# Turning softmax probabilities by halves of 49 rows, in two goes of six blocks

## The chip, the cores and the metric

The kernel runs on one core of one Trainium2 chip. Its time is the device time of one execution in microseconds (us); lower is better. The core has TensorE (PE: matrix products out of SBUF into the eight PSUM banks; PEld is its loading of weights), VectorE (DVE), ScalarE (ACT), GpSimd (POOL, which does not read PSUM) and the DMA queues. Each engine works through its own instructions in order and meets the others at semaphores.

## What is computed

Four layers one after the other on x of 32 images, 56 x 56 pixels, 96 channels, float32. The first and third are of no matter here (a depthwise convolution along the pixels with two products; a 7 x 7 depthwise convolution that is part of the third layer). The second and the fourth are the same transformer block on windows of 7 x 7 pixels with six heads of 16 channels:

```python
h = _ln(x, g1, b1)
h = jnp.roll(h, shift=(-SHIFT, -SHIFT), axis=(1, 2))
h = h.reshape(B, nHw, WS, nWw, WS, C).transpose(0, 1, 3, 2, 4, 5).reshape(B * nHw * nWw, WS * WS, C)
q, k, v = jnp.moveaxis((h @ w_qkv + b_qkv).reshape(-1, N, 3, nh, hd), 2, 0)
attn = jax.nn.softmax(jnp.einsum('wqhd,wkhd->whqk', q, k) * scale, axis=-1)
out = jnp.einsum('whqk,wkhd->wqhd', attn, v).reshape(-1, N, C) @ w_proj + b_proj
...
x = shortcut + out
h2 = _ln(x, g2, b2)
return x + jax.nn.gelu(h2 @ w_fc1 + b_fc1, approximate=False) @ w_fc2 + b_fc2
```

The third layer has the attention too, with a bias and a mask, and no second half.

## The kernel before

The program is a row of passes: `scan_pass` (first layer), `window_pass` for "L1" (second layer, here called the second pass), `conv_pass`, `window_pass` for "L2" (third layer) and `window_pass` for "L3" (fourth layer, here called the fourth pass). In `window_pass` the flag `mlp` is true for L1 and L3; the change touches only what stands under it.

A chunk is one row of eight windows of one image, 8 x 49 = 392 pixels; there are 32 x 8 = 256 chunks in a pass. All four engines go over the chunks in step (`over_chunks`, with 24 steps to a turn of the hardware loop), each with a step function written out by hand: `mlp_step` for L1 and L3. A step is software-pipelined: in step t, TensorE makes keys, queries, values and scores of chunk t (`st.f`), turns the probabilities, takes heads and the projection of chunk t-1 (`st.k`), the hidden products of chunk t-2 (`st.m`) and the output products of chunk t-3 (`st.n`). `st.wait(name, lag)` waits until a semaphore has counted the chunk `lag` back. `hold` puts such a wait on an instruction of its own.

The windows are worked in pairs, the even window on partitions 0 to 48 and the odd one on 64 to 112, so that a tile spans `SPAN` = 113 rows. The probabilities stand in PR as 113 query rows by 24 head slots of 64 columns: window pair by window pair (four), six heads each. The product of probabilities and values (`heads`, L1069) needs them with the keys on the partitions, so TensorE turns them against the identity (`turn`, L1006): a block is two heads of a window pair, 113 rows by 113 columns, loaded as weights, while 113 columns of the identity stream through. Twelve blocks make a chunk (`PAIRS` x `G`, 4 x 3). They are turned in three lots of four, a lot to one PSUM bank: lot 0 to bank 4, lot 1 to bank 5, lot 2 to bank 4 again, which waits for `pt0`, the copy of lot 0 to the tile PT. VectorE makes that copy (L1388), ScalarE those of lots 1 and 2 (L1235). `probs0` and `probs1` are the two halves of the exponential (L1251), twelve head slots each.

TensorE's step around it is: keys and queries (L1013), output products 0 and 1 (`output`, L1105; each waits for the low parts that GpSimd makes, L1501), turn of lot 0, the sums of squares (`variances`, L990), output product 2, turns of lots 1 and 2, the spreading of 1/std to the channels (`spread`, L1000; it waits for ScalarE's logarithm L1226 and exponential L1230 of the variances), values (L1028), in L3 the turn to pixels (L1097), heads (L1069), two hidden products (L1013), scores (L1052), the turn of the heads (L1076), the third hidden product and the projection (L1087). Bank 5 is also that of the heads and of the projection, bank 4 that of the turned heads.

## Time and profile before

| what | us |
|---|---|
| runs | 11234.27, 11250.2, 11244.17 |
| median | 11244.17 |
| profiled execution, its own time | 11245.42 |
| its span in the trace | 11243.6 |
| TensorE busy in the span | 10697.9 (95%) |
| ScalarE, VectorE, GpSimd busy | 7724.4 (69%), 7313.1 (65%), 5856.8 (52%) |

The mean granted clock of TensorE is 0.978. In the views, a row of a timeline gives the start and the length of a group in us from the span's start; the length of a group of TensorE instructions overlaps with the next group, since products are pipelined, so starts are the better measure. A product in float32 that is no turn appears as two rows (x48 for 24 instructions), a turn as one. "113*96" before a shape is the rows and columns of the array that are used.

### The profile page before, as it was taken

Reading aid. Unit: us, or ns where it says so; the run is one execution under the profiler, and the core shown is the slowest. Engines: PE = TensorE matmul, PEld = TensorE weight load, DVE = VectorE, ACT = ScalarE, POOL = GpSimd, SP = SyncE. Lnnn points to the kernel's source line nnn. Section 1 sums busy time; section 2 is a strip of 40 time slices with the busy share of each in tenths; the row PEclk is TensorE's granted clock in tenths of the full one; section 3 lists DMA queues with packets and bytes.
Section 4 is the critical chain, followed back from the end, with each engine's and each line's share of the span. In section 5 each row is a group of like instructions: output and inputs, shape, how many; then the busy total and the mean of one; then the engine's idle time right before and its main releaser. Section 6 shows DMA issues by size and latency. Waiting matters only on the chain. (4 is left out here: it accounts for less than half of the span.)

```text
span 11243.6 us, 395055 instructions
## 1 busy us (share of the span) xinstructions
PE 10697.9 (95%) x160084; PEld 8550.1 (76%) x160084; DVE 7313.1 (65%) x12431; ACT 7724.4 (69%) x13429; POOL 5856.8 (52%) x7492
## 2 busy tenths in 40 slices
PE   6999998999999999998989999998999999999999
PEld 4666666777777777777767777776888888888888
DVE  4555555777777777773467676766666666666666
ACT  4555554777777777774357676765777777777777
POOL 2333334777777777771034444443555555555555
PEclk9999998999999999999989999998999999999999
DMA  2111111222222222225633333332111111111110
GB/s 60 51 46 51 46 42 36 52 52 52 52 52 52 52 52 52 52 52 173 215 80 79 76 80 76 80 77 51 26 26 26 25 25 26 26 26 26 25 25 23
DMA packets 1105555, 617.35 MB, mean 55 GB/s; under 512 B 864635, under 2 KB 1076550, under 8 KB 1099688
## 3 DMA queue, kind: packets, MB, share of 16 engines
q1 hardware_dynamic: 1091368, 552.46, 20.4%
q10 hardware_dynamic: 12288, 38.54, 1.0%
q8 instruction: 1317, 21.58, 0.8%
q14 instruction: 582, 4.77, 0.1%
HBM read 307.18 MB, written 282.75 MB: 52 GB/s over the span
## 5 line engine op out<-in xcount | busy, mean ns | idle before, releaser
L1501 POOL TENSOR_TENSOR L_HdL<-L_Hd,L_HdH 128x392 fp32r<-128x392 f32 x1536 | 1576.8, 1027 | 280.9 <-POOL L_HdH L1499 279.3
L1006 PE MATMUL banks<-L_ident,L_PR 113*113 113x113 f32 x9216 | 1201.7, 267 | 1.2 <-DVE L_X L1407 0.7
L1006 PEld LDWEIGHTS banks<-L_ident,L_PR 113*113 113x113 f32 x9216 | 1143.6, 180 | 67.2 <-DVE L_X L1407 9.8
L1235 ACT COPY L_PT<-banks 113x452 f32<-113x452 f32 x1792 | 886.1, 538 | 397.7 <-PE banks L1006 394.3
L1251 ACT ACTIVATE L_PR<-L_SX 113x588 f32<-113x588 f32 x1536 | 1088.5, 709 | 86.5 <-DVE L_SX L1379 10.2
L1069 PE MATMUL banks<-L_VB,L_PT 113*49 113x34 f32 x36864 | 1064.8, 213 | 2.0 <-ACT L_PT L1235 1.0
L1373 DVE TENSOR_REDUCE L_MX<-banks 113x12 f32<-113x588 f32 x1024 | 783.6, 765 | 433.5 <-PE banks L1052 433.5
L1069 PEld LDWEIGHTS banks<-L_VB,L_PT 113*49 113x49 f32 x36864 | 1016.7, 126 | 25.5 <-issue 1.8
L1490 POOL CAST L_XNH<-L_XN 97x392 fp32r<-97x392 f32 x512 | 448.6, 876 | 1105.4 <-DVE L_XN L1420 1105.4
L1499 POOL CAST L_HdH<-L_Hd 128x392 fp32r<-128x392 f32 x1536 | 784.6, 511 | 459.9 <-issue 425.6
L1052 PEld LDWEIGHTS banks<-L_KX,L_QT 32*49 32x49 f32 x36864 | 565.1, 119 | 333.9 <-issue 331.8
L1549 POOL COPY L_XN<-L_XR 96x392 f32<-96x392 f32 x256 | 149.6, 584 | 1278.3 <-DMA L_XR<-L_norm 1193.8
L1379 DVE TENSOR_TENSOR L_SX<-banks,L_MX 113x588 f32<-113x588 f32 x1024 | 788.8, 770 | 35.3
L1052 PE MATMUL banks<-L_KX,L_QT 32*49 32x98 f32 x36864 | 726.1, 249 | 50.1 <-issue 49.1
L1028 PE MATMUL banks<-L_Wv,L_XN 97*49 97x48 f32 x24576 | 730.2, 213 | 0.0
L1105 PE MATMUL banks<-L_HdH,L_W2H 128*97 128x392 f32 x1536 | 593.6, 386 | 121.2 <-POOL L_HdL L1501 121.1
L1087 PE MATMUL banks<-L_OT,L_Wp 97*97 97x392 f32 x1536 | 691.8, 532 | 14.5 <-ACT L_OT L1282 1.1
L1028 PEld LDWEIGHTS banks<-L_Wv,L_XN 97*49 97x49 f32 x24576 | 634.5, 127 | 78.2 <-issue 3.0
L1286 ACT ACT_TABLE_LOAD x512 | 656.9, 1283 | 9.4
L1274 ACT ACT_TABLE_LOAD x512 | 656.9, 1283 | 9.2
L1388 DVE COPY L_PT<-banks 113x452 f32<-113x452 f32 x512 | 321.9, 629 | 515.1 <-PE banks L1006 515.1
L1439 DVE SCALAR_TENSOR_TENSOR L_X<-banks,L_fc2b,L_X 97x392 f32<-97x392 f32 x512 | 320.3, 626 | 515.1 <-PE banks L1105 515.1
(249 smaller groups left out, 28455.0 us busy)
## 6 DMA issues: line engine op xcount, KB each, us to landing
L_X<-after_L SPq DMA_DIRECT2D x768, 147.0 KB
after_L<-L_X SPq DMA_DIRECT2D x512, 147.0 KB
conv_T<-L_norm_by_phase SPq DMA_DIRECT2D x96, 512.0 KB, 3.3
L_norm_by_phase<-L_XP SPq DMA_DIRECT2D x512, 84.0 KB, 2.1
scan_XT<-in_x SPq DMA_DIRECT2D x32, 1176.0 KB, 6.9
L_norm<-L_XA SPq DMA_DIRECT2D x256, 147.0 KB, 1.9
L_conv<-conv_D ACTq DMA_DIRECT2D x96, 392.0 KB, 3.0
L_XR<-L_norm SPq DMA_DIRECT2D x256, 147.0 KB, 2.4
```

The source lines that it names most:

```text
L1006: mm = pe.transpose(bank(TURN[a])[0:SPAN, (k % 4) * SPAN:(k % 4 + 1) * SPAN], PR[:, st.v if lag else st.u, 2 * k:2 * k + 2, :].rearrange(" ...
L1028: mm = pe.matmul(bank(VALUES_BANK)[HALF * e:HALF * e + TOK, q * G * HD:(q + 1) * G * HD], XN[:, st.u, q * TOK:(q + 1) * TOK], Wv[0:C + 1, ...
L1052: mm = pe.matmul(bank(g)[p0:p0 + TOK, q // 2 * 2 * TOK:(q // 2 + 1) * 2 * TOK].rearrange("c (e k) -> c e k", e=2), QT[rows, st.u, q * TOK: ...
L1069: mm = pe.matmul(bank(HEADS_BANK)[p0:p0 + TOK, col:col + VW], PT[:, st.v, q // 2 * G + g, p0:p0 + TOK], VB[:, st.v, q, g, :], start=True, ...
L1087: pe.matmul(bank(PROJ_BANK)[0:C + 1, 0:CH], Wp[0:C + 1, :], OT[:, st.v], start=mlp, stop=True).then_inc(s["proj"], 1)
L1235: act.copy(PT[:, st.v if lag else st.u, 4 * a:4 * a + 4, :].rearrange("c k q -> c (k q)"), bank(TURN[a])[0:SPAN, 0:4 * SPAN]).then_inc(s[f ...
L1251: act.activation(PR[:, u, a, 0:TOK], SX[:, u, a], ACT.Exp).then_inc(s[f"probs{half}"], 1)
L1274: act.preload_act_table_set(GELU)
L1373: dve.tensor_reduce(mx, src, AX.X, ALU.max).then_inc(s[f"rowmax{half}"], 1)
L1379: dve.tensor_tensor(dst, src, spread, ALU.subtract).then_inc(s[f"centred{half}"], 1)
L1499: pool.tensor_copy(HdH[:, u, j].bitcast(F32R), Hd[:, u, j]).then_inc(s[f"hd_high_{j}"], 1)
L1501: pool.tensor_tensor(HdL[:, u, j].bitcast(F32R), Hd[:, u, j], HdH[:, u, j], ALU.subtract).then_inc(s[f"hd_parts_{j}"], 1)
```

## The change

In L1 and L3 `turn` gives way to `turn_halves`. Each block of 113 x 113 is turned as two: the 49 rows of the even window, from partitions 0 to 48, into bank 4, and the 49 rows of the odd window, from partitions 64 to 112, into bank 5. Each has 49 rows and 113 columns of PR as weights and 49 columns of the identity as stream, and writes 49 columns. There are two goes of six blocks, twelve turns each, the first behind `probs0`, the second behind `probs1` and `pt0`, in place of lots of four, four and four. Both goes use both banks. Each go has one copy, 588 elements on each of 113 partitions in place of 452: VectorE's for the first, ScalarE's for the second, written around the unused columns of PT (`by_window`). The wait for `x1` moves ahead of the first go, since it writes bank 5 now. The waits for `probs0` and `pt0` become held waits. L2 keeps `turn` with three lots.

```diff
+        names += [f"{n}{a}" for n in ("turned", "pt") for a in range(2 if mlp else 3)] + ["heads", "rsum", "normed", "heads_t", "ot", "proj", "x1"]
+        HALVES = slice(4, 6)
+        HP = PAIRS * G // 2
+        def turned_halves():
+            return PS[0:SPAN, HALVES, 0:HP * TOK].rearrange("c e (k q) -> c e k q", q=TOK)
+        def by_window(t):
+            return bass.AP(t.tensor, t.offset, [t.ap[0], [HALF, 2], [SPAN, HP], [1, TOK]])
...
+                def turn_halves(st, a):
+                    for k in range(HP * a, HP * a + HP):
+                        for e in range(2):
+                            rows = slice(HALF * e, HALF * e + TOK)
+                            mm = pe.transpose(PS[0:SPAN, HALVES.start + e, (k % HP) * TOK:(k % HP + 1) * TOK],
+                                              PR[rows, st.v, 2 * k:2 * k + 2, :].rearrange("c h k -> c (h k)")[:, 0:SPAN], ident[rows, rows])
+                    mm.then_inc(s[f"turned{a}"], 1)
...
                     if st.k:
-                        st.wait("probs0", 1)
-                        turn(st, 0)
+                        st.wait("x1", 2)
+                        hold(pe, s["probs0"], st.value(1), passed)
+                        turn_halves(st, 0)
                     if normed:
                         variances(st)
                     if st.n:
                         output(st, 2).then_inc(s["fc2"], 1)
                     if st.k:
-
-                        st.wait("x1", 2)
                         st.wait("probs1", 1)
-                        turn(st, 1)
-                        st.wait("pt0", 1)
-                        turn(st, 2)
+                        hold(pe, s["pt0"], st.value(1), passed)
+                        turn_halves(st, 1)
...
+                def pt_halves(st, a):
+                    st.wait(f"turned{a}", 1)
+                    act.copy(by_window(PT[:, st.v, HP * a:HP * a + HP, :]), turned_halves()).then_inc(s[f"pt{a}"], 1)
...
-                        pt_copy(st, 1)
-                        pt_copy(st, 2)
+                        pt_halves(st, 1)
```

VectorE's copy is changed in the same way (`pt_copy(st, 0)` to `pt_halves(st, 0)`). Lines move by some twenty: `turn_halves` is L1025 in the changed kernel, the output products L1124, the variances L1000, the spreading L1010.

TensorE in a step of L3, from the last row of output product 1 to the spreading, as it stands before (HdH and W2L are high and low parts of the hidden layer and its weights, SQ the squares, J the averaging matrix, RS the 1/std, PICK the spreading matrix):

```order
L1105 MATMUL banks<-L_HdH,L_W2L 97x392
L1006 MATMUL banks<-L_ident,L_PR 113x113 x4
L687 REGISTER_ALU
L990 MATMUL banks<-L_SQ,L_J 32x98 x8
L1105 MATMUL banks<-L_HdH,L_W2H 97x392
L1105 MATMUL banks<-L_HdL,L_W2H 97x392
L1105 MATMUL banks<-L_HdH,L_W2L 97x392
L1006 MATMUL banks<-L_ident,L_PR 113x113 x8
L1000 MATMUL banks<-L_RS,L_PICK 96x98 x8
```

The same place on TensorE in the changed kernel:

```order
L1124 MATMUL banks<-L_HdH,L_W2L 97x392
L1025 MATMUL banks<-L_ident,L_PR 113x49 x12
L687 REGISTER_ALU
L1000 MATMUL banks<-L_SQ,L_J 32x98 x8
L1124 MATMUL banks<-L_HdH,L_W2H 97x392
L1124 MATMUL banks<-L_HdL,L_W2H 97x392
L1124 MATMUL banks<-L_HdH,L_W2L 97x392
L1025 MATMUL banks<-L_ident,L_PR 113x49 x12
L1010 MATMUL banks<-L_RS,L_PICK 96x98 x8
```

Four turns ahead of the variances and eight behind the last output product have become twelve of half the height and 49 columns out at each place; nothing else has moved.

ScalarE in the same step, from the logarithm to the rounding of XN2, before:

```order
L1226 ACTIVATE L_LV<-banks,L_eps 64x392
L1230 ACTIVATE L_RS<-L_LV 64x392
L1235 COPY L_PT<-banks 113x452 x2
L1264 CAST L_XN2H<-L_XN 97x392
L1244 COPY L_VB<-banks 49x24x16
```

and in the changed kernel:

```order
L1243 ACTIVATE L_LV<-banks,L_eps 64x392
L1247 ACTIVATE L_RS<-L_LV 64x392
L1272 COPY L_PT<-banks 113x2x6x49
L1284 CAST L_XN2H<-L_XN 97x392
L1261 COPY L_VB<-banks 49x24x16
```

Two copies have become one with more elements, at the same place.

## Rows read from the trace of the kernel before

**Rows 1.** The page, busy time, share of the span and instructions of each engine:

```profile
PE 10697.9 (95%) x160084; PEld 8550.1 (76%) x160084; DVE 7313.1 (65%) x12431; ACT 7724.4 (69%) x13429; POOL 5856.8 (52%) x7492
```

**Rows 2.** Windows: us, busy of PE, PEld, DVE, ACT, POOL, clock, DMA, GB/s:

```profile
2800.00:5100.00 2300.00, 2183.75 (x38968) 1796.08 (x38955) 1660.14 (x2864) 1728.89 (x2876) 1664.57 (x2330) 0.99 0.24 52
...
8000.00:11243.00 3243.00, 3195.18 (x52345) 2740.07 (x52343) 2147.03 (x3634) 2515.51 (x4376) 1759.08 (x2185) 0.99 0.10 25
```

**Rows 3.** Waits, 8100 to 11100 (L3): total us, times, longest:

```profile
ACT L_XN2H L1264 <- DVE L_XN L1417: 198.9, 226, 0.9
...
PEld banks L1013 <- issue: 116.3, 226, 4.0
...
PEld banks L1087 <- ACT L_OT L1282: 78.7, 226, 0.4
```

**Rows 4.** Waits, 2200 to 5000 (L1):

```profile
PEld banks L1105 <- POOL L_HdL L1501: 174.2, 210, 1.2
```

**Rows 5.** Timeline of one chunk in L3: start, length, engine, line, operation, count:

```profile
9004.04 0.34 PE L1105 MATMUL banks<-L_HdH,L_W2L 128*97 128x392 f32 x1
...
9004.22 0.56 PE L1006 MATMUL banks<-L_ident,L_PR 113*113 113x113 f32 x4
...
9004.70 0.87 PE L990 MATMUL banks<-L_SQ,L_J 96*32 96x98 f32 x16
...
9005.62 0.58 ACT L1226 ACTIVATE L_LV<-banks,L_eps 64x392 f32<-64x392 f32 x1 [0.18 <-PE banks L990]
...
9005.95 0.34 PE L1105 MATMUL banks<-L_HdH,L_W2L 128*97 128x392 f32 x1
...
9006.13 0.95 PE L1006 MATMUL banks<-L_ident,L_PR 113*113 113x113 f32 x8
9006.24 0.53 ACT L1230 ACTIVATE L_RS<-L_LV 64x392 f32<-64x392 f32 x1
...
9007.02 0.92 PE L1000 MATMUL banks<-L_RS,L_PICK 32*96 32x98 f32 x16
...
9007.87 0.94 PE L1028 MATMUL banks<-L_Wv,L_XN 97*49 97x48 f32 x32
...
9009.80 1.37 PE L1069 MATMUL banks<-L_VB,L_PT 113*49 113x34 f32 x48
```

**Rows 6.** Timeline of one chunk in L1:

```profile
4006.77 1.03 POOL L1501 TENSOR_TENSOR L_HdL<-L_Hd,L_HdH 128x392 fp32r<-128x392 f32 x1 [0.18 <-POOL L_HdH L1499]
...
4007.85 0.42 PE L1105 MATMUL banks<-L_HdH,L_W2H 128*97 128x392 f32 x1 [0.45 <-POOL L_HdL L1501]
...
4010.20 0.34 PE L1105 MATMUL banks<-L_HdH,L_W2L 128*97 128x392 f32 x1
...
4010.50 0.53 ACT L1230 ACTIVATE L_RS<-L_LV 96x392 f32<-96x392 f32 x1
...
4011.26 0.93 PE L1000 MATMUL banks<-L_RS,L_PICK 32*96 32x98 f32 x24
```

**Rows 7.** Timeline of PE in L3, windows that end at 9007.10 and at 9007.20:

```profile
9006.83 0.26 PE L1006 MATMUL banks<-L_ident,L_PR 113*113 113x113 f32 x1
9007.02 0.33 PE L1000 MATMUL banks<-L_RS,L_PICK 32*96 32x98 f32 x2
...
9007.02 0.41 PE L1000 MATMUL banks<-L_RS,L_PICK 32*96 32x98 f32 x4
```

**Rows 8.** Weight loads by line, 8100 to 11100: ns min/median/max, array rows*columns:

```profile
L1006 PEld LDWEIGHTS banks<-L_ident,L_PR x2708: 174/179/313, 8101.2 to 11091.3; 113*113 113x113 f32 x194
...
L1069 PEld LDWEIGHTS banks<-L_VB,L_PT x10848: 121/126/126, 8105.0 to 11095.5; 113*49 113x49 f32 x198
...
L1076 PEld LDWEIGHTS banks<-L_ident,L_O x904: 123/126/128, 8108.5 to 11098.1; 113*96 113x96 f32 x181
...
L1000 PEld LDWEIGHTS banks<-L_RS,L_PICK x3616: 154/159/161, 8102.3 to 11092.2; 32*96 32x96 f32 x191
```

**Rows 9.** The page, costliest groups: busy us, mean ns, idle before:

```profile
L1379 DVE TENSOR_TENSOR L_SX<-banks,L_MX 113x588 f32<-113x588 f32 x1024 | 788.8, 770 | 35.3
```

More of the change, by code:

```diff
@@ L839, in window_pass @@
                  "centred0", "centred1", "probs0", "probs1"]
-        names += ["turned0", "turned1", "turned2", "pt0", "pt1", "pt2", "heads", "rsum", "normed", "heads_t", "ot", "proj", "x1"]
+        names += [f"{n}{a}" for n in ("turned", "pt") for a in range(2 if mlp else 3)] + ["heads", "rsum", "normed", "heads_t", "ot", "proj", "x1"]
         if mlp:
@@ L1060, in heads @@
                     st.wait("pt1", 1)
-                    st.wait("pt2", 1)
                     if not mlp:
+                        st.wait("pt2", 1)
                         st.wait("ot", 2)
@@ L1384, in centre, with pt_halves @@
                     subtract(st, half)
-                def pt_copy(st, a):
+                def pt_halves(st, a):
                     st.wait(f"turned{a}", 1)
-                    dve.tensor_copy(PT[:, st.v, 4 * a:4 * a + 4, :].rearrange("c k q -> c (k q)"), bank(TURN[a])[0:SPAN, 0:4 * SPAN]).then_inc(s[f"pt{a}"], 1)
+                    dve.tensor_copy(by_window(PT[:, st.v, HP * a:HP * a + HP, :]), turned_halves()).then_inc(s[f"pt{a}"], 1)
                 def over_sums(st):
@@ L1432, in mlp_step @@
                     if st.k:
-                        pt_copy(st, 0)
+                        pt_halves(st, 0)
                     if st.n:
```

## The prediction

> **What bounds the kernel now.** I read the page's busy shares first: TensorE is busy 95% of the span, the next engine 69% [rows 1]. By stage, the two passes that the change touches hold it at 0.95 and 0.99 of the time, at a granted clock of 0.99, which is the 2.4 GHz level [rows 2]. Whatever TensorE takes longer or shorter on these passes therefore counts, unless a wait takes the difference. So I read the waits next. In the fourth pass every wait of TensorE is a short one behind its own work: for the turned heads (78.7 us over 226 chunks) and before the keys (116.3 us) [rows 3]; the view has no wait of it around the turning of the probabilities. In the second pass there is one more: the output product waits for GpSimd's low parts, 174.2 us in 210 waits [rows 4]. The timeline shows that this is a ring: GpSimd ends the second low part at 4007.80 (6.77 + 1.03), TensorE starts the output product at 4007.85, goes through the first turn, the variances, the output's last third, the second turn and the spreading (start 4011.26), VectorE makes XN from the spread factors, and GpSimd's splitting starts again from XN [rows 6]. Both turns lie inside that ring, so in the second pass, too, their time is the chunk's time.
>
> How much room is behind the turns? In the fourth pass (rows 5) the variances start at 9004.70, the logarithm at 9005.62, the exponential ends at 9006.77, and the spreading, which waits for it, starts at 9007.02. A semaphore takes about 0.06 us here (4007.80 to 4007.85 in rows 6), so the spreading has 0.19 us of room. In the second pass the exponential ends at 4011.03 against 4011.26, the same. **The second turn can be shortened by 0.2 us at most before the chain of logarithm and exponential ends last**; the first turn stands ahead of the variances, so it moves that chain with it at full price.
>
> **What the turns cost now.** From the start of the last output product to the start of what follows: first turn 9004.04 to 9004.70, 0.66 us; second turn 9005.95 to 9007.02, 1.07 us [rows 5]; in the second pass the second turn takes 1.06 (4010.20 to 4011.26) [rows 6]. Together 1.73 us for each chunk. Eight turns take 0.95 us as one group with the last one lasting 0.26, so they start (0.95 - 0.26) / 7 = 0.099 us apart [rows 5, 8].
>
> What sets these 0.099 us? Two things could: the 113 columns that stream, or the 113 columns of probabilities that are loaded as weights. The change cuts the stream to 49 columns and leaves the load at 113. So this is the question on which all hangs. Load times grow with the number of columns: 49 columns 126 ns, 96 columns 159, 113 columns 179 [rows 8], which is (179 - 126) / 64 = 0.83 ns for a column, about 0.094 us for 113. The group that turns values by heads separates load from stream: L1069 loads 49 columns and streams 34; its 48 rows take 1.37 us, the last 212 ns, so pairs (two column halves side by side) start (1.37 - 0.21) / 47 x 2 = 0.049 us apart [rows 5, 8]. L1028 loads 49 and streams 48: (0.94 - 0.21) / 31 x 2 = 0.047 us [rows 5, 8]. A stream a third shorter has brought nothing: **where the load is longer than the stream, the load sets the pace.** A pair of halves then starts 0.10 us after the last pair, no faster than a whole block now.
>
> The Trainium skill says the same of a load by itself: "TensorE: Matmul & The Clock Gate", section "LDWEIGHTS (loading the stationary operand)", gives a time by columns and none by rows, so loading 49 rows in place of 113 saves nothing. Rows 8 agree (32 rows with 96 columns take 159 ns, 113 rows with 49 columns 126).
>
> Do two halves run side by side at all? The nearest row is L1000, 32 rows high, in two row groups by turns: 16 products take 0.92 us in all and the first 4 of them 0.41 [rows 5, 7], so a further two take (0.92 - 0.41) / 6 = 0.085 us. That is what one stream of 98 columns takes at 0.099 us for 113, and no more than one load of 96 at 0.83 ns for a column: two loads and two streams go in the time of one. I take the halves to be side by side.
>
> **What a change of the array's shape costs.** A turn of now and the output product ahead of it use the array in one shape (113 and 128 rows, up to 113 and 97 columns), and the first turn starts 0.18 us after the last product, which is that product's own pace [rows 5]. Where the shape changes, a gap stands: the last turn starts at 9006.83, L1000 at 9007.02, 0.19 where 0.10 is the pace, so 0.09 more [rows 7]. Then the first load is bare: the first two products last 0.33 in place of some 0.24, and after four the busy time is 0.41, so the second pair starts 0.41 - 0.24 = 0.17 after the first where the pace is 0.08. That is 0.09 more for a load of 96 columns; I take 0.09 for 113 too. Both are paid today behind each turn. The change adds a pair of them ahead of each turn, since 49 rows in half of the array is another shape than the 128 rows of the output product.
>
> The Trainium skill has this as a rule that speaks against the change: "TensorEngine Tiling (Array Packing)", section "Key Properties", says that changing the mode, not only the tile, drains the engine. It gives no price; without the rule a go would cost what the rival on the shape below says, and rows 7 agree with the rule.
>
> **The sum.** A go of six blocks after the change: product's pace 0.18 + gap 0.09, first pair to second 0.10 + 0.09, four more starts 0.40, then the last pair's 49 columns 0.05 and the gap to the next shape 0.09: 1.00 us. Both goes have six blocks: 2.00 us against 1.73, **0.27 us more for each chunk**; the first go +0.34, the second -0.07. The spreading's room shrinks from 0.19 to about 0.12, so the exponential stays just ahead. 32 images of 8 window rows are 256 chunks in each of the two passes, 512 in all: 138 us.
>
> Beside the path:
> - VectorE's copy grows from 452 to 588 elements, about 0.77 us, as L1379 takes for 588 elements out of such banks [rows 9]. It starts at the first go's end: the last pair starts at 9004.04 + 0.86 = 9004.90, and with a product's 0.24 that is 9005.15; the copy ends near 9005.95. The second go, which waits for it now because both goes use the same two banks, starts near 9006.13 + 0.34 + 0.09 = 9006.55. Some 0.6 us of the variances and the output product cover it, and it would cost its excess if that were gone.
> - ScalarE makes one copy of 588 elements for two of 452, which is less work. XN2H behind it waits for VectorE, 198.9 us in 226 [rows 3]: nothing gained.
> - The wait for x1 moves from the second turn to ahead of the first go. That x1 is two chunks back, made by VectorE's residual right behind the projection of the step before, while TensorE still has keys, queries and the output to do. Nothing. If it came late, the first go and all behind it in TensorE's order would stand, the ring of the second pass with them.
> - The separate waits for probs0 and pt0 (a semaphore instruction each, where the first load now carries the wait) have no row at this place. Below: nothing, since the gap for the shape covers them. Above: the largest wait of that sort, before the keys, 116.3 us in 226, which is 0.51 each [rows 3], other causes included; half of that for the two goes together would give 0.27 + 0.25 = 0.52 a chunk, 266 us. I take nothing, since neither is late (the turn starts at its product's pace today), and keep the bound for the range.
>
> 11,244 + 138 = **11,382 us**. The profiled execution took 11,245.4 us for a span of 11,243.6, so span and median of the runs (11,244.2) may be used alike.
>
> **Rivals.**
> - *The load of a half is fast; the change is quicker.* For: L1076 loads 96 columns of a turn in 126 ns where L1000 needs 159 for 96 [rows 8], so some turns load at nearly twice the rate. Against: L1006, the same tile and the same 113 columns, has 179. If pairs go at pace p, a go costs 0.41 + 6p (the bare first load shrinks too): 0.71 us at 0.05. First go +0.05, second -0.36; but the exponential then ends last, and the spreading can come only 0.14 us earlier than today. 512 x 0.14 = 72 us: 11,172 us. It decides below p = 0.076 us, where a go costs half of 1.73. The Trainium skill's "Theoretical Speedup" in "TensorEngine Tiling (Array Packing)" would have it so: up to twice the rate for 64 rows or fewer; rows 7 show that for loads of equal length, rows 5 deny it where the load outlasts the stream.
> - *No gap for this shape.* For: the columns stay at 113. Against: from L1006 to L1000 only the rows change shape as well, and the gap is there. A go: 0.18 + 0.50 + 0.14 = 0.82; first +0.16, second -0.25; again the exponential ends last, 0.03 us earlier than today: 11,229 us.
> - *Halves not side by side.* No row shows a turn of under 64 rows. A go of 12 single turns: 0.27 + 0.19 + 1.00 + 0.14 = 1.60, two 3.20, 1.47 more, 753 us: 11,997 us.
> - The rest: a lower clock by an emptier array, or waits beyond the bound; slower by more than the range.
>
> **Chances.** Forecast 0.63, with its own range 11,290 to 11,510 (the load never bare, 0.27 - 0.18 = 0.09 a chunk; the waits at their bound). Fast load 0.11, no gap 0.10, one after another 0.09, the rest 0.07. To leave out no more than 2 in 10 the range takes in the case without a gap for the most part: 11,215 to 11,510. A measurement of this kernel tells 0.2%, 22 us, from no change: faster 0.14, same 0.07, slower 0.79.
>
> **What would show it.** In the profile after, the first load of a turn starting about 0.27 us after the last output product, pairs 0.10 us apart with loads still near 175 ns, products far shorter in stream; the first go some 1.0 us from product to variances, and the chunk 0.27 us longer in both passes, the third pass untouched. Pairs at 0.05 us, or a wait of the spreading on the exponential, would show the first rival; starts 0.10 us apart one by one the third.

## The result and the profile after

The changed kernel takes **11,416.3 us** (median of 4 runs, 11,411.5 to 11,421.2) against 11,243.0 us of the kernel before (4 runs, 11,234.3 to 11,250.2): a ratio of 1.0152, 95% interval 1.0141 to 1.0164. That is 173 us more. I had predicted 138 us more, 11,382 us, in a range from 11,215 to 11,510. The profiled execution took 11,421.2 us for a span of 11,419.4.

The page of the kernel after: span, busy time by engine, and the groups of the half turns and of VectorE's copy (busy us, mean ns of one, idle time before it). It answers to [rows 1] and [rows 9].

```profile
span 11419.4 us, 407351 instructions
PE 10861.5 (95%) x166228; PEld 8500.2 (74%) x166228; DVE 7372.2 (65%) x12431; ACT 7576.6 (66%) x12917; POOL 5855.9 (51%) x7492
...
L1025 PEld LDWEIGHTS banks<-L_ident,L_PR 49*113 49x113 f32 x12288 | 694.8, 177 | 294.4 <-issue 294.1
L1408 DVE COPY L_PT<-banks 113x588 f32<-113x588 f32 x512 | 394.8, 771 | 698.9 <-PE banks L1025 698.9
```

6144 more products (two for each of 12 blocks in place of one, 512 times), and TensorE is busy 164 us more, close to the 173 that the kernel lost. The load of a half still takes 177 ns, as a whole block's did [rows 8]. The copy's 771 ns is the 0.77 us taken from [rows 9].

One chunk of the fourth pass, timeline of the kernel after; L1124 is the output product, L1025 the turn, L1000 the variances, L1010 the spreading. It answers to [rows 5].

```profile
9012.36 0.34 PE L1124 MATMUL banks<-L_HdH,L_W2L 128*97 128x392 f32 x1
9012.63 0.67 PEld L1025 LDWEIGHTS banks<-L_ident,L_PR 49*113 49x113 f32 x12 [0.28 <-issue]
9012.63 0.79 PE L1025 MATMUL banks<-L_ident,L_PR 49*113 49x49 f32 x12
9013.35 0.87 PE L1000 MATMUL banks<-L_SQ,L_J 96*32 96x98 f32 x16
9013.47 0.77 DVE L1408 COPY L_PT<-banks 113x588 f32<-113x588 f32 x1 [0.82 <-PE banks L1025]
...
9014.59 0.34 PE L1124 MATMUL banks<-L_HdH,L_W2L 128*97 128x392 f32 x1
9014.87 0.80 PE L1025 MATMUL banks<-L_ident,L_PR 49*113 49x49 f32 x12
9014.89 0.53 ACT L1247 ACTIVATE L_RS<-L_LV 64x392 f32<-64x392 f32 x1
...
9015.59 0.92 PE L1010 MATMUL banks<-L_RS,L_PICK 32*96 32x98 f32 x16
```

Read from product to what follows: first go 9012.36 to 9013.35, 0.99 us, where it was 0.66; second go 9014.59 to 9015.59, 1.00, where it was 1.07. The first turn starts 0.27 after the product (0.18 before). Over all chunks of the pass the medians are 0.995 and 0.997. The exponential ends at 9015.42 (14.89 + 0.53) and the spreading starts at 9015.59.

The same timeline, TensorE alone, cut at 9012.8 and at 9012.9, so that the count says how many turns had started:

```profile
9012.63 0.40 PE L1025 MATMUL banks<-L_ident,L_PR 49*113 49x49 f32 x4
...
9012.63 0.50 PE L1025 MATMUL banks<-L_ident,L_PR 49*113 49x49 f32 x6
```

Two more turns, one pair, cost 0.10 us. So the halves of a pair run side by side (their starts are 0.003 us apart in the records) and pairs go at the pace of a whole block before.

Windows of both passes (us, busy PE, PEld, DVE, ACT, POOL, granted clock, DMA, GB/s), which answer to [rows 2]:

```profile
2800.00:5100.00 2300.00, 2183.85 (x40022) 1734.79 (x40020) 1638.79 (x2784) 1620.14 (x2612) 1618.50 (x2263) 0.98 0.24 51
8000.00:11243.00 3243.00, 3208.15 (x54717) 2665.42 (x54715) 2146.37 (x3598) 2415.65 (x4080) 1738.64 (x2160) 0.99 0.10 25
```

TensorE remains as full as before. The waits of 8200 to 11200 have one new line (total us, times, longest), 0.28 us ahead of each go:

```profile
PEld banks L1025 <- issue: 126.7, 444, 0.5
```

**Where the 173 us are.** From one spreading to the next, the median chunk of the second pass grew from 12.606 to 12.939 us (+0.333), that of the fourth from 13.070 to 13.310 (+0.240). There are 254 such distances in each pass: 85 + 61 = 146 us. Of the other 27, 20 lie in the second pass and 6 in the fourth, nearly all of it at the turns of the hardware loop (every 24 chunks): the time that all chunks together took beyond 254 median ones rose from 43.0 to 63.3 us in the second pass and from 45.6 to 51.9 in the fourth.

### The profile page after: what moved, and what is told of

Read it like the earlier page. It is cut to its first block and busy times, and to the rows that moved or that the text cites. A ratio compares the mean times of both kernels' runs of the same rounds, so it can differ in the third digit from the quotient of the medians.

```text
span 11419.4 us, 407351 instructions
## 1 busy us (share of the span) xinstructions
PE 10861.5 (95%) x166228; PEld 8500.2 (74%) x166228; DVE 7372.2 (65%) x12431; ACT 7576.6 (66%) x12917; POOL 5855.9 (51%) x7492
## 5 line engine op out<-in xcount | busy, mean ns | idle before, releaser
L1025 PEld LDWEIGHTS banks<-L_ident,L_PR 49*113 49x113 f32 x12288 | 694.8, 177 | 294.4 <-issue 294.1
L1408 DVE COPY L_PT<-banks 113x588 f32<-113x588 f32 x512 | 394.8, 771 | 698.9 <-PE banks L1025 698.9
L1025 PE MATMUL banks<-L_ident,L_PR 49*113 49x49 f32 x12288 | 823.0, 267 | 0.9 <-ACT L_PR L1268 0.7
L1124 PE MATMUL banks<-L_HdH,L_W2H 128*97 128x392 f32 x1536 | 594.5, 387 | 133.1 <-POOL L_HdL L1521 133.1
L1243 ACT ACTIVATE L_LV<-banks,L_eps 96x392 f32<-96x392 f32 (+2 forms) x523 | 305.4, 584 | 519.5 <-PE banks L1000 519.5
L1252 ACT COPY L_PT<-banks 113x452 f32<-113x452 f32 x768 | 387.6, 538 | 394.0 <-PE banks L1016 391.4
```

The costliest lines, as they stand in the source:

```text
L1025: mm = pe.transpose(PS[0:SPAN, HALVES.start + e, (k % HP) * TOK:(k % HP + 1) * TOK], PR[rows, st.v, 2 * k:2 * k + 2, :].rearrange("c h k - ...
L1124: mm = pe.matmul(bank(6)[0:C + 1, 0:CH], wt[:, j, :].bitcast(F32R), xt[:, st.v, j].bitcast(F32R), start=(j == 0 and n == 0), stop=(j == HB ...
```

## The experiments

All twelve stand against the kernel before, run on the same chip in the same session. The medians of all of them are in the table, read from the traces in the same way: "chunk" is the distance between two spreadings, a go lasts from the start of the last output product to the start of what follows it.

| kernel | time, us | chunk, 2nd pass | chunk, 4th pass | first go (2nd/4th) | second go (2nd/4th) | load, ns |
|---|---|---|---|---|---|---|
| before | 11,243 | 12.606 | 13.070 | 0.667 / 0.686 | 1.063 | 179 |
| after | 11,416 | 12.939 | 13.310 | 0.995 | 0.996 | 176 |
| cols96 | 11,215 | 12.624 | 12.882 | 0.684 | 0.893 / 0.878 | 123 |
| cols112 | 11,235 | 12.663 | 12.928 | 0.732 | 0.894 / 0.880 | 131 |
| cols114 | 11,240 | 12.674 | 12.941 | 0.738 | 0.892 / 0.882 | 133 |
| cols127 | 11,452 | 13.015 | 13.450 | 1.065 | 1.066 | 187 |
| cols128 | 11,256 | 12.710 | 12.968 | 0.773 | 0.894 / 0.880 | 138 |
| full66 | 11,301 | 12.805 | 13.078 | 0.865 / 0.885 | 0.887 / 0.879 | 179 |
| half48 | 11,386 | 12.806 | 13.304 | 0.795 | 1.194 | 176 |
| even_first | 11,679 | 13.276 | 13.795 | 1.230 | 1.233 | 176 |
| full128 | 11,236 | 12.605 | 13.030 | 0.660 | 1.050 | 141 |
| between | 11,182 | 12.353 | 13.060 | (moved) / 0.667 | 1.061 | 179 |
| half210_128 | 11,161 | 12.463 | 12.880 | 0.526 / 0.546 | 1.023 | 138 |
| best | 11,141 | 12.349 | 12.880 | (moved) / 0.543 | 1.022 | 138 |

In the fourth pass of before, one half of the first goes took 0.667 us and the other 0.686, and in that of full66 it is alike (0.865 and 0.885).

### Fewer and more columns of the load: cols96 and cols128

In `turn_halves` the number of columns of PR that are loaded, and of partitions written, changes. cols96 leaves out the last 17 keys of the second head, and cols112 below the last one, so their output is another one; their copies take as many partitions fewer, and PT is filled with ones before.

```diff
-mm = pe.transpose(PS[0:SPAN, HALVES.start + e, ...], PR[rows, ...][:, 0:SPAN], ident[rows, rows])
+mm = pe.transpose(PS[0:96, HALVES.start + e, ...], PR[rows, ...][:, 0:96], ident[rows, rows])
```

> The changed kernel, with 96 in place of 113 columns of the probabilities loaded for each half in L1 and L3 (the last 17 keys of the second head are left out; PT is filled with ones before). Theory (a half's weight load sets the pace of the turns): the pace of the pairs, 0.096 us in the changed kernel, falls with the load, while the stream of 49 columns stays as it is. If these columns load at the rate of L1000 (159 ns for 96), pairs come every 0.082 us: a go is 0.08 us shorter, 0.17 a chunk in L3, 11,340 to 11,380 us. If they load at the rate of the turned heads L1076 (126 ns for 96), pairs come every 0.05 us, 0.27 less a go. Rival (the stream, or a fixed cost of issue, sets the pace): pairs stay at 0.096 us and the time at 11,416.

Measured: 11,214.5 us in one run, before 11,243.6. The load dropped to 123 ns, far below what 17 fewer columns are worth at 0.83 ns, and the first go to 0.684 us. The expectation's 0.27 us less a go came near (0.31), its rival (a pace set by the stream or by issue) did not hold.

```diff
-mm = pe.transpose(PS[0:SPAN, HALVES.start + e, ...], PR[rows, ...][:, 0:SPAN], ident[rows, rows])
+mm = pe.transpose(PS[0:128, HALVES.start + e, ...], PR[rows, ...], ident[rows, rows])
```

> The changed kernel, with 128 in place of 113 columns loaded for each half in L1 and L3 (the 15 further rows of the bank are not read). Theory A (load by columns at 0.83 ns each): load near 187 ns, pairs 0.107 to 0.11 us apart, each go 0.07 longer, 0.14 a chunk: 11,460 to 11,490 us. Theory B (turns load at the double rate where the count of columns is even, as the 96 of L1076 at 126 ns; 113 is slow because it is odd): load near 140 ns, pairs about 0.06 us apart, each go some 0.2 shorter than 0.995; the spreading then waits for the exponential, and the time is 11,200 to 11,290 us.

Measured: 11,256.3 us (11,247.6 to 11,261.8), ratio 1.0011 (1.0002 to 1.0021). **More columns, and 160 us faster than the changed kernel.** Weight loads of the half turns from 8200 to 11000, ns min/median/max, of after, of cols96 and of cols128:

```profile
L1025 PEld LDWEIGHTS banks<-L_ident,L_PR x4968: 170/176/312, 8204.8 to 10994.2; 49*113 49x113 f32 x199
```

```profile
L1025 PEld LDWEIGHTS banks<-L_ident,L_PR x5136: 119/123/194, 8202.5 to 10997.9; 49*96 49x96 f32 x198
```

```profile
L1025 PEld LDWEIGHTS banks<-L_ident,L_PR x5088: 134/138/226, 8202.0 to 10991.0; 49*128 49x128 f32 x196
```

The load's time is not a matter of how many columns alone. The timeline of cols128 shows what that does to a go:

```profile
9009.16 0.34 PE L1124 MATMUL banks<-L_HdH,L_W2L 128*97 128x392 f32 x1
...
9009.43 0.57 PE L1025 MATMUL banks<-L_ident,L_PR 49*128 49x49 f32 x12
...
9009.94 0.87 PE L1000 MATMUL banks<-L_SQ,L_J 96*32 96x98 f32 x16
...
9011.17 0.34 PE L1124 MATMUL banks<-L_HdH,L_W2L 128*97 128x392 f32 x1
...
9011.45 0.57 PE L1025 MATMUL banks<-L_ident,L_PR 49*128 49x49 f32 x12
...
9012.05 0.76 PEld L1010 LDWEIGHTS banks<-L_RS,L_PICK 32*96 32x96 f32 x16 [0.16 <-ACT L_RS L1247]
9012.06 0.92 PE L1010 MATMUL banks<-L_RS,L_PICK 32*96 32x98 f32 x16
```

`PEld` in the last rows is the weight load of the spreading. The twelve turns have the same gap of 0.27 in front, and take 0.57 in place of 0.79. The first go falls from 0.99 to 0.78, the second only from 1.00 to 0.89, because now the spreading waits for the exponential (`ACT L_RS`). That is the limit of 0.2 us that the prediction drew from [rows 5].

### What count is fast: cols112, cols114, cols127

The same line with 112, 114 and 127 columns.

> The changed kernel with 112 in place of 113 columns loaded for each half in L1 and L3 (the last key of the second head is left out; PT is filled with ones before). 96 columns took 123 ns to load, 128 took 138, 113 took 176. Theory A (an odd count loads at the slow rate): 112 columns load in about 130 ns, pairs 0.05 us apart, 11,220 to 11,260 us. Theory B (the double rate needs a multiple of 32 columns): 112 columns load in about 175 ns, pairs 0.096 apart, 11,416 us.

Measured: 11,234.9 us in one run, before 11,238.6; load 131 ns. So the fast load takes no multiple of 32.

> The changed kernel with one more column loaded by each half turn: 114 in place of 113, everything else as it is; the column's result is not read, so nothing is left out. The runs with 96, 112 and 128 columns loaded in 123, 131 and 138 ns, the changed kernel's 113 columns in 176. All three fast counts are multiples of 16, so it is open whether it takes that or an even count. Theory 'even': 114 is fast: on the line through the three, 131 + 2 x 0.47, about 132 ns; first go 0.73 to 0.75 us, chunk 12.67 in the second pass and 12.93 in the fourth, time 11,235 to 11,245 us. Theory 'multiple of 16' (or of 4 or 8): 114 is slow, 177 to 180 ns, goes of 1.00 us, time about 11,418 us.

Measured: 11,240.2 us in one run, before 11,246.2. One column more than the changed kernel, and 176 us less. Loads of cols114:

```profile
L1025 PEld LDWEIGHTS banks<-L_ident,L_PR x5088: 128/133/214, 8208.4 to 10996.8; 49*114 49x114 f32 x196
```

> The changed kernel with 127 columns loaded by each half turn in place of 113, everything else as it is; the results of the columns past 113 are not read, so nothing is left out. 96, 112, 114 and 128 columns were fast, 113 slow. Theory 'an odd count loads at the slow rate': 0.83 ns for each of 14 more columns than 113, so 176 + 12 = about 188 ns a load, pairs about 0.108 us apart, a go of 1.05 to 1.07 us, time 11,440 to 11,480 us. Theory '113 alone, or its remainder to a multiple of 16, is slow for another reason': 127 is fast, 137 to 138 ns, and the time is that of the run with 128 columns, about 11,250 us.

Measured: 11,451.6 us in one run, before 11,230.2; goes of 1.065 us. Loads of cols127:

```profile
L1025 PEld LDWEIGHTS banks<-L_ident,L_PR x4908: 182/187/334, 8201.0 to 10993.6; 49*127 49x127 f32 x197
```

What follows: the load of a float32 turn has two rates, and here **an odd number of columns took the slow one** (113: 176 ns, 127: 187; 11 / 14 = 0.8 ns for a column) and an even number the fast one (96, 112, 114, 128: 123, 131, 133, 138; 15 / 32 = 0.47 ns for a column). Between 113 and 114 columns lie 43 ns. Only two odd counts have been tried.

The pace follows the load one for one. With the stream at 49 columns throughout, pairs start 0.047, 0.055, 0.056, 0.062, 0.099 and 0.111 us apart where a load takes 123, 131, 133, 138, 176 and 187 ns: 76 to 77 ns less than the load each time.

### Whole blocks in the new order: full66

The two goes of six with their waits and copies, but each block turned whole; three blocks in each bank, 678 elements for a copy in place of 588:

```diff
 for k in range(HP * a, HP * a + HP):
-    for e in range(2):
-        rows = slice(HALF * e, HALF * e + TOK)
-        mm = pe.transpose(PS[0:SPAN, HALVES.start + e, (k % HP) * TOK:(k % HP + 1) * TOK], PR[rows, ...], ident[rows, rows])
+    j = k % HP
+    mm = pe.transpose(PS[0:SPAN, HALVES.start + j // 3, (j % 3) * SPAN:(j % 3 + 1) * SPAN], PR[:, ...], ident[0:SPAN, 0:SPAN])
```

> The split of the change without its halves: full blocks of 113 x 113 in two goes of six, three blocks to a bank, two copies (678 elements each). Theory (the loss in the changed kernel is the added gap and bare load ahead of each go, 0.09 + 0.04 each, plus two blocks moved ahead of the variances, which counts in full only in L1, where VectorE's chain from the output to XN ends last behind a shorter second go): the first go 0.86 us and the second 0.86, no gap ahead of them; L1 chunk +0.20 over the kernel before, L3 chunk between 0 and +0.05: 11,290 to 11,310 us. Rival (the split costs nothing, all of the loss is from the halves): 11,243.

Measured: 11,300.9 us (11,299.3 to 11,304.2), ratio 1.0053 (1.0037 to 1.0070). First go of full66:

```profile
9018.12 0.36 PE L1123 MATMUL banks<-L_HdH,L_W2L 128*97 128x392 f32 x1
...
9018.32 0.76 PE L1024 MATMUL banks<-L_ident,L_PR 113*113 113x113 f32 x6
...
9019.01 0.87 PE L1000 MATMUL banks<-L_SQ,L_J 96*32 96x98 f32 x16
```

Six whole blocks need 0.87 to 0.89 us against 0.995 for six pairs of halves: the halves cost 0.11 to 0.13 us a go more, of which 0.09 is the later start (0.27 against 0.18 after the product, medians 0.271 and 0.178). The held waits are in this kernel too, and its turns start at the product's pace: they cost nothing.

It also shows where the split of goes alone leads. In the fourth pass the first go's +0.199 and the second's -0.184 nearly cancel (chunk +0.008). In the second pass the chunk is +0.199: the first go's price is paid, the second's saving isn't returned.

### Another split of the blocks: half48

```diff
+GO = ((0, 4), (4, 12))
-for k in range(HP * a, HP * a + HP):
+for k in range(*GO[a]):
```

> The halves of the change, but in goes of four and eight blocks as before (the second holds 392 columns in each bank), still two copies (392 and 784 elements). Theory (in L1 the chunk grew by 0.333 and not by 0.26, because the shorter second go is not given back: VectorE's X2, KX, XN2, XN end last): first go 0.80 us, second 1.19, L1 chunk +0.26 over the kernel before, L3 chunk +0.24 as in the changed kernel, 11,395 us. Rival (the split has no part in it): L1 chunk +0.33 still, 11,416.

Measured: 11,386.4 us (11,370.9 to 11,401.4), ratio 1.0133 (1.0116 to 1.0150). The goes, 0.795 and 1.194, sum to 1.989 like 0.995 and 0.996, and the fourth pass has the same chunk as the changed kernel (13.304 against 13.310). The second pass's is 0.133 shorter, although the sum is the same. So in that pass a microsecond in the first go and one in the second are not worth the same. The expectation had both goes' +0.13 count, +0.26; the chunk grew by 0.200. The reason stands under the second pass below.

### The order of the halves: even_first

```diff
-for k in range(HP * a, HP * a + HP):
-    for e in range(2):
+for e in range(2):
+    for k in range(HP * a, HP * a + HP):
```

> The changed kernel with the order inside a go turned round: the six halves of the even windows first, then the six of the odd windows, so that neighbours load into the same rows of the array. Theory (alternate halves run side by side because they are in different rows, as L1000 shows): now they come one by one 0.096 us apart, a go takes about 1.55 us in place of 0.995, 1.1 us more a chunk, 11,950 to 12,050 us. Rival (the pace is that of one go whatever the order, since the engine sorts loads itself): 11,416 us.

Measured: 11,678.9 us in one run, before 11,237.0; a go takes 1.23 us. First go of even_first:

```profile
9015.52 0.34 PE L1124 MATMUL banks<-L_HdH,L_W2L 128*97 128x392 f32 x1
...
9015.79 1.03 PE L1025 MATMUL banks<-L_ident,L_PR 49*113 49x49 f32 x12
...
9016.75 0.87 PE L1000 MATMUL banks<-L_SQ,L_J 96*32 96x98 f32 x16
```

Neither theory had this number. One after another twelve turns would need some 1.6 us for a go, side by side 1.0. The records don't name the half, but by their medians the twelve starts fall into two rows of six with the same steps: 0, 0.135, 0.235, 0.334, 0.433 and 0.532 us, which I read as the even windows', and 0.240, 0.376, 0.475, 0.574, 0.673 and 0.772, the odd ones'. Each row goes at the pace of pairs, the go ends 0.24 later than with pairs, and between 0.24 and 0.53 both rows run at once. So the halves do run together, and for the full gain they have to alternate; why the second row starts 0.24 late is not shown.

One rival stays open: in every kernel with halves the even windows go to bank 4 and the odd ones to bank 5, so the row half of the array and the bank change together, and no run separates them. A change of bank alone brings nothing to whole blocks: in full66 the third and the fourth block, in different banks, start 0.099 us apart like the others.

### Fast loads without halves: full128

The kernel before, with 128 columns of PR loaded in place of 113 in the second and fourth pass:

```diff
-mm = pe.transpose(bank(TURN[a])[0:SPAN, ...], PR[:, ...][:, 0:SPAN], ident[0:SPAN, 0:SPAN])
+mm = pe.transpose(bank(TURN[a])[0:128, ...], PR[:, ...], ident[0:SPAN, 0:SPAN])
```

> The kernel before with 128 in place of 113 columns loaded for a full block in L1 and L3, all else as it was. Loads should fall from 179 to about 140 ns. Theory (of a full block the stream of 113 columns takes as long as the slow load of 113, so the fast load brings nothing there, and pays only together with a short stream): starts 0.097 us apart, 11,243 us, within 0.1%. Rival (the load alone sets the pace of the kernel before): starts 0.06 us apart, 0.4 us less a chunk before other waits, under 11,150 us.

Measured: 11,236.3 us in one run, before 11,237.0, as the theory had it. Its loads:

```profile
L1007 PEld LDWEIGHTS banks<-L_ident,L_PR x2532: 137/141/231, 8205.2 to 10991.3; 113*128 113x128 f32 x195
```

Loads of 141 ns in place of 179, and goes of 0.660 and 1.050 in place of 0.667 and 1.063: the second pass's chunk stays, and the fourth's is 0.04 shorter. With whole blocks the stream of 113 columns sets nearly the same pace (0.097 us) that the load of 113 did (0.099). **Each change alone brings nothing or a loss; both together bring the turns' time down** (0.773 and 0.88 to 0.89 in cols128 against 0.667 and 1.063 before).

### Moving the first turn: between

The kernel before; in the second pass the first turn (with its wait for `probs0`) stands between output products 0 and 1 in place of behind 1:

```diff
 output(st, 0)
-output(st, 1)
+st.wait("probs0", 1)
+turn(st, 0)
+output(st, 1)
-st.wait("probs0", 1)
-turn(st, 0)
```

> The kernel before with one move in L1 alone: the turn of lot 0 stands between output products 0 and 1, where TensorE waits for GpSimd's low parts, and no longer behind them in the ring. Theory (the ring GpSimd, output, turns, variances, spreading, XN sets the L1 chunk): the chunk gets 0.3 to 0.4 us shorter, 11,150 to 11,170 us. Rival (L1 is bound by TensorE's own sum): no change, 11,243.

Measured: 11,181.7 us (11,179.4 to 11,188.8), ratio 0.9951 (0.9934 to 0.9968). Timeline of the second pass in between (L1006 is the turn, L1105 the output product, L1505 GpSimd's low part of the hidden layer):

```profile
4007.43 1.03 POOL L1505 TENSOR_TENSOR L_HdL<-L_Hd,L_HdH 128x392 fp32r<-128x392 f32 x1 [0.18 <-POOL L_HdH L1503]
...
4008.15 0.65 PE L1006 MATMUL banks<-L_ident,L_PR 113*113 113x113 f32 x4
...
4008.57 0.41 PE L1105 MATMUL banks<-L_HdH,L_W2H 128*97 128x392 f32 x1
...
4009.10 1.01 POOL L1505 TENSOR_TENSOR L_HdL<-L_Hd,L_HdH 128x392 fp32r<-128x392 f32 x1 [0.18 <-POOL L_HdH L1503]
...
4010.17 0.16 PEld L1105 LDWEIGHTS banks<-L_HdH,L_W2H 128*97 128x97 f32 x1 [0.24 <-POOL L_HdL L1505]
```

The turn fills the time in which TensorE waited for the second low part (until 4008.46), and the chunk is 0.253 shorter. That bears out the ring of [rows 6], though the 0.3 to 0.4 that I expected, and its 11,150 to 11,170 us, were too much. Not the whole go is won: TensorE now waits for the probabilities ahead of the turn, and for the third low part ahead of output product 2.

### Two blocks first, ten after, with 128 columns: half210_128, and best

half210_128 is the changed kernel with `GO = ((0, 2), (2, 12))` as in half48 and 128 columns as in cols128. In best the first go stands in the second pass between output products 0 and 1, as in between.

> Halves as in the change, loads of 128 columns, goes of two and ten blocks, two copies (196 and 980 elements). From the runs so far a pair costs 0.055 us, a go of two blocks 0.55, of ten 0.99, together 1.54 against 1.73 us before. Theory: L3 chunk -0.19 us against the kernel before, L1 chunk -0.12 (the first go counts in full, the rest is under VectorE's chain), 11,165 to 11,190 us. Rival (the second copy, now near 1.0 us on ScalarE, or its wait, ends last): L3 chunk as before or longer, 11,243 us and up.

Measured: 11,161.0 us (11,147.1 to 11,164.0), ratio 0.9929 (0.9912 to 0.9946). Timeline of its fourth pass (L1126 output, L1027 turns, L1001 variances, L1011 spreading):

```profile
9012.32 0.34 PE L1126 MATMUL banks<-L_HdH,L_W2L 128*97 128x392 f32 x1
...
9012.59 0.33 PE L1027 MATMUL banks<-L_ident,L_PR 49*128 49x49 f32 x4
...
9012.84 0.87 PE L1001 MATMUL banks<-L_SQ,L_J 96*32 96x98 f32 x16
...
9014.08 0.34 PE L1126 MATMUL banks<-L_HdH,L_W2L 128*97 128x392 f32 x1
...
9014.36 0.82 PE L1027 MATMUL banks<-L_ident,L_PR 49*128 49x49 f32 x20
...
9015.11 0.93 PE L1011 MATMUL banks<-L_RS,L_PICK 32*96 32x98 f32 x16
```

That is 4 us below the 11,165 to 11,190 expected. The first go is 0.52 and the second 1.03, no wait for the exponential in between: the blocks that stand in the second go hide the logarithm and the exponential, and those of the first are few.

> The two gains together: halves with loads of 128 columns in goes of two and ten blocks, and in L1 the first go between output products 0 and 1. Theory (the two add up, since the one shortens the ring after GpSimd's parts and the other the second go): L3 chunk -0.19 us against the kernel before as in the run with two and ten, L1 chunk -0.30 to -0.40, 11,090 to 11,130 us. Rival (with the ring cut, TensorE's own sum or VectorE's chain binds L1, and the gaps on both sides of the first go are paid): L1 chunk about -0.25 as with the move alone, 11,130 to 11,150 us.

Measured: **11,141.4 us** (11,138.4 to 11,153.4), ratio 0.9917 (0.9899 to 0.9934), faster than both kernels. The two gains did not add up, against the theory; the rival's 11,130 to 11,150 us held, for a reason that it did not name. In the fourth pass it keeps the gain of half210_128 (12.880). In the second it stands at 12.349, no better than between alone (12.353). Timeline of its second pass:

```profile
4012.82 0.33 PE L1027 MATMUL banks<-L_ident,L_PR 49*128 49x49 f32 x4
...
4013.77 1.02 POOL L1528 TENSOR_TENSOR L_HdL<-L_Hd,L_HdH 128x392 fp32r<-128x392 f32 x1 [0.18 <-POOL L_HdH L1526]
...
4014.85 0.42 PE L1126 MATMUL banks<-L_HdH,L_W2H 128*97 128x392 f32 x1
```

GpSimd ends the third low part at 4014.79 and output product 2 starts at 4014.85. GpSimd's own row, from the splitting of XN to this low part, ends last now, so a shorter turn ahead of it is waiting time, not gain.

## Why the prediction was right, and where its sizes were off

**The load sets the pace: right.** A pair goes every 0.10 us (0.096 + 0.003), as taken, with a stream of 49 columns; the load stayed at 176 ns. The 0.83 ns a column came from a line through products (49 columns) and a turn (113), on which the 96 columns of [rows 8] don't lie (0.70 ns a column up to them, 1.18 from there); that the odd counts of the turn have nearly that slope, 0.8, is luck. But the reason behind the first rival, that some turns load at nearly twice the rate, was right as well, only not for 113 columns. I had the row of that (L1076, 96 columns in 126 ns [rows 8]) and the row against it (L1006, 113 columns in 179), and took them for two kinds of turn. They were one kind with an even and an odd count. cols114 is that rival come true: pairs 0.056 us apart where it took 0.05, a go of 0.738 where it worked out 0.71, and in the fourth pass 0.129 a chunk less than before, by the exponential's room, where it gave 0.14. That it stands at 11,240 us and not at the rival's 11,172 is for the most part the second pass, whose chunk is 0.068 longer than before (+17 us where the rival had -36): the first go is paid there and the second returns nothing (below).

**Side by side: right.** The starts within a pair are 0.003 us apart; even_first shows that the order matters.

**The gap for the shape: right.** Lead of the first turn 0.271 against 0.178: 0.093, where 0.09 was taken. full66, with whole blocks behind the same held waits, has 0.178. That also settles the bound for the waits: nothing, as taken. This agrees with the Trainium skill, "TensorEngine Tiling (Array Packing)", section "Key Properties", by which a change of mode drains the engine.

**Inside a go the terms were off both ways and cancelled.** First pair to second 0.135 where 0.19 was taken, so the bare load costs 0.04, not 0.09. I had carried over L1000's figure; its stream is twice as long, but that this makes the difference is not shown. Last pair to the next shape 0.19 where 0.14 was taken: the stream is shorter than the load but does not let the next shape in earlier than before. Sum: 0.271 + 0.135 + 4 x 0.099 + 0.19 = 0.99, against 1.00 predicted.

**The fourth pass: +0.240 a chunk where 0.27 was predicted.** By the medians of the goes it is (0.995 + 0.997) - (0.686 + 1.063) = 0.243. The one chunk of [rows 5] had a first go of the shorter kind, 0.66. The spreading kept its room, 9015.42 to 9015.59, as foreseen.

**The second pass: +0.333 where 0.27 was predicted. This term was mis-sized.** I gave the second go's saving of 0.07 back in both passes. The ring of [rows 6] has two ways from the last output product to XN, and I followed one. Timeline of VectorE in the second pass after the change, with TensorE's two rows:

```profile
3992.37 0.34 PE L1124 MATMUL banks<-L_HdH,L_W2L 128*97 128x392 f32 x1
...
3992.89 0.62 DVE L1459 SCALAR_TENSOR_TENSOR L_X<-banks,L_fc2b,L_X 97x392 f32<-97x392 f32 x1 [0.88 <-PE banks L1124]
...
3993.36 0.93 PE L1010 MATMUL banks<-L_RS,L_PICK 32*96 32x98 f32 x24
3993.43 1.15 DVE L1357 TENSOR_SCALAR L_KX<-banks,L_mask 96x392 f32<-96x392 f32 x2
...
3994.50 0.55 DVE L1437 TENSOR_TENSOR L_XN<-L_X,banks 96x392 f32<-96x392 f32 x1
3994.97 0.55 DVE L1440 TENSOR_TENSOR L_XN<-L_X,banks 96x392 f32<-96x392 f32 x1
```

The last XN of the chunk of [rows 6], before the change:

```profile
4012.79 0.55 DVE L1420 TENSOR_TENSOR L_XN<-L_X,banks 96x392 f32<-96x392 f32 x1
```

From the output product on VectorE does the residual, the masked keys and XN without a gap, 3992.89 to the last XN, which starts at 3994.97: 2.60 us after the product. The spreading starts at 3993.36 and ends at 3994.29, 0.21 before the first XN (3994.50), which also waits for it. Before the change the last XN started at 4012.79, 2.59 after the product of 4010.20; the spreading had ended at 4012.19, 0.13 before the first XN (4012.32). So the second go went from 1.06 to 0.99, and XN came no earlier. VectorE's row ends last there, and only the first go's +0.33 is left, which is what was measured.

The medians of all kernels say the same. Wherever the second go takes 0.89 to 1.07 us, the last XN of the second pass starts 2.60 us after the output product, in before and after alike; with 1.19 (half48) it starts 2.66 after it and with 1.23 (even_first) 2.70. So the spreading begins to set XN's time only with a go longer than before, and a shorter one returns nothing. The chunks follow: full66 has +0.199 for a first go of +0.198, half48 +0.200 for +0.13 in the first go and 0.06 in XN, and cols127, whose two goes are each 0.07 longer than after, is 0.076 longer in the second pass and 0.140 in the fourth. No run moved VectorE's row itself.

**At the turns of the hardware loop: +27 us, not foreseen.** Where the loop turns, TensorE stands still for about 4 us, and then its granted clock is at the 1.2 GHz level for a while. Windows just behind such a turn, before the change and after it (same columns as above):

```profile
3515.00:3540.00 25.00, 21.19 (x314) 16.96 (x302) 14.16 (x25) 15.71 (x27) 15.57 (x23) 0.93 0.24 50
```

```profile
3570.00:3595.00 25.00, 21.51 (x287) 17.38 (x287) 11.38 (x19) 10.93 (x19) 12.65 (x20) 0.66 0.21 45
```

Over 2200 to 5000 the clock records show 34 us at the lower level before and 96 after; five of the nine stretches lasted 14 to 17 us, where none lasted over 6.8 before. The extra 62 us at half the rate are worth up to 31 us, and 20 were measured in that pass. The long stretches are these 20 us: in the changed kernel's second pass the two chunks at a loop turn take 4.4 us beyond two ordinary ones in each of the four turns where the lower level lasted 3.4 us (before, 4.4 to 4.9), and 7.9 to 9.2 in the five where it lasted 14 or 17. That is some 4.5 us for each, 22 in all. Among the experiments there is an order: the kernels with whole blocks (full128, full66, between) have 38 to 44 us there, those with halves of fast loads 48 to 68, those with halves of slow loads 75 (cols127), 109 (half48) and 123 (even_first), each from one trace. Why the clock stays down longer with half turns is not shown, and in the fourth pass (8200 to 11000) the changed kernel has no more of it (41 us) than the one before (44). This stays open.

**Sum.** 85 (second pass; 69 predicted) + 61 (fourth; 69 predicted) + 27 (loop turns; 0 predicted) = 173 us.

**Not tried:** cutting the stream to 49 columns, or the load, without halves. A turn takes a square identity as stream, so the one can't be had without the other.

## What to carry to other kernels

Packing two half-height products side by side gains only as far as the stream was the limit: read the weight load's time beside the stream's, and count a change of shape (0.09 us here) at both ends of each group. Before such a step, look at whether the number of columns that a float32 turn loads is odd: one column more, never read, was worth 176 us here. Where an engine saves time ahead of a meeting point, follow every engine that comes to it (VectorE's chain here, GpSimd's in the last experiment), and put what has room where one waits: two blocks and ten, not six and six.

## What the runs showed of the hardware that I had not expected

- A float32 turn loads its weights in 123, 131, 133 and 138 ns for 96, 112, 114 and 128 columns, and in 176 and 187 ns for 113 and 127. The number of rows (49 or 113) changes it by 3 ns. The Trainium skill, "TensorE: Matmul & The Clock Gate", section "Weight-path perf modes — Fast Weight Load (FWL) and DoubleRow", has a faster load for 128 weights that aren't float32; here 96, 112 and 114 float32 weights were fast as well, so that rule doesn't explain it.
- With loads of 114 and 96 columns a pair of half turns goes every 0.056 and 0.047 us, 49 columns of stream each, where a whole block takes 0.10.
- Two row halves of the array work together all along only if their turns alternate: 0.995 us for a go in turns, 1.23 us with all of one half first, where the second half starts 0.24 us late.
- In the second pass the TensorE clock stayed at its lower level for up to 17 us behind a stand of 4 us in the kernels whose half turns had slow loads, up to 14 us in those with fast ones (6.8 at most in cols112, cols128 and half210_128), and 6.8 us at most in the four with whole blocks.
